# A Mamba stage with its last sums carried into the next round, two sets of semaphores, one block of Silu, and GpSimd two products ahead

## The reference, cut to what matters

```
hidden = layernorm(residual)
xin, z = split(hidden @ in_w.T)
xc = silu(causal_conv4(xin) + cb)
dtr, B, C = split(xc @ xp_w.T)
dt = softplus(dtr @ dtp_w.T + dtp_b)
h_t = exp(dt_t * A) * h_{t-1} + (dt_t * xc_t) * B_t     # A = -exp(A_log), for each state n
y_t = sum_n h_t[n] * C_t[n] + xc_t * D
residual = residual + (y * silu(z)) @ out_w.T
```

## Time and profile before

| what | us |
|---|---|
| median of three timed runs | 8238.78 (8215.06 to 8246.3) |
| the profiled execution | 8203.76 |
| its span | 8201.8 |
| busy in the span: TensorE, VectorE, ScalarE, GpSimd | 6408.0, 6500.0, 4681.8, 4525.0 |
| the Mamba rounds, from first to last scan and read-out | 107.87 to about 4081 |

### The profile page before, as it was taken

The page is one execution under the profiler, slowest core; times in us unless marked ns, Lnnn a source line. Parts: engine busy times, 40 slices in busy tenths (PEclk is TensorE's granted clock), DMA queues, the critical chain, the costliest instruction groups (busy, mean ns, idle before and its releaser), DMA issues. The chain is left out here.

```text
span 8201.8 us, 94294 instructions
## 1 busy us (share of the span) xinstructions
PE 6408.0 (78%) x25989; PEld 3374.8 (41%) x25989; DVE 6500.0 (79%) x15305; ACT 4681.8 (57%) x9323; POOL 4525.0 (55%) x2829
## 2 busy tenths in 40 slices
PE   5888888888888888888788867777556777777755
PEld 2333333333333333333355545555434444444522
DVE  5999989999899999999855558988667666666657
ACT  4666666666666666666555533433326666666633
POOL 4888888888888888888732335545211222222200
PEclk9999999999999999999977878888656777778755
DMA  5333333433433333343310047777310000000011
GB/s 183 143 154 152 149 140 151 161 139 155 156 142 154 149 152 145 146 161 138 147 33 27 21 129 209 215 210 211 104 45 14 10 10 10 10 10 10 7 34 36
DMA packets 373870, 896.58 MB, mean 109 GB/s; under 512 B 28169, under 2 KB 270214, under 8 KB 307110
## 3 DMA queue, kind: packets, MB, share of 16 engines
q1 hardware_dynamic: 332646, 692.64, 22.5%
q0 software_dynamic: 40960, 201.36, 8.5%
HBM read 850.57 MB, written 56.77 MB: 111 GB/s over the span
## 5 line engine op out<-in xcount | busy, mean ns | idle before, releaser
L365 POOL TENSOR_TENSOR mb_dBu<-mb_dtu,mb_rows_b 128x1024 f32<-128x1024 f32 x1027 | 2401.7, 2356 | 143.7 <-POOLq L63 98.9
L379 DVE TENSOR_TENSOR_SCAN mb_bank<-mb_bank,mb_dBu 128x1024 f32<-128x1024 f32 x704 | 1611.0, 2288 | 141.2 <-PEq L63 107.6
L350 ACT ACTIVATE mb_bank<-mb_dt,mb_a_neg 128x508 f32<-128x508 f32 x2050 | 1312.8, 671 | 2.3
L419 PE MATMUL mb_bank<-mb_hcd,ident 128*128 128x512 f32 x2560 | 1213.2, 607 | 25.1 <-DVE mb_hcd L393 25.0
L419 PE MATMUL mb_bank<-mb_hcp,ident 128*128 128x512 f32 x1280 | 856.3, 806 | 344.5 <-POOL mb_hcp L402 344.5
L402 POOL TENSOR_TENSOR mb_hcp<-mb_hs,mb_rows_c 128x1024 f32<-128x1024 f32 x320 | 750.9, 2347 | 479.8 <-DVE mb_hs L379 445.8
L393 DVE TENSOR_TENSOR mb_hcd<-mb_bank,mb_rows_c 128x1024 f32<-128x1024 f32 x704 | 861.8, 1224 | 32.3 <-PE mb_bank L419 0.7
L419 PEld LDWEIGHTS mb_bank<-mb_hcd,ident 128*128 128x128 f32 x2560 | 499.9, 200 | 753.9 <-issue 632.6
L379 DVE TENSOR_TENSOR_SCAN mb_hs<-mb_bank,mb_dBu 128x1024 f32<-128x1024 f32 x320 | 731.1, 2285 | 83.8 <-ACT mb_bank L350 83.8
L1523 POOL DMA_INDIRECT ex_rows<-in_ex_table,ex_idx x512 | 489.8, 957 | 523.9 <-DVE ex_idx L1519 310.4
L419 PEld LDWEIGHTS mb_bank<-mb_hcp,ident 128*128 128x128 f32 x1280 | 304.8, 253 | 777.8 <-POOL mb_hcp L402 412.6
(11 more groups left out here) (369 smaller groups left out, 12892.1 us busy)
## 6 DMA issues: line engine op xcount, KB each, us to landing
mb_rows_b<-bc_rows SPq DMA_DIRECT2D x259, 1024.0 KB, 7.6
mb_rows_c<-bc_rows SPq DMA_DIRECT2D x258, 1024.0 KB, 6.8
stream<-mb_r_post SPq DMA_DIRECT2D x69, 256.0 KB, 2.7
mb_r_tok<-stream SPq DMA_DIRECT2D x67, 256.0 KB, 2.7
mb_r_old<-stream SPq DMA_DIRECT2D x65, 256.0 KB, 2.8
ex_rows<-in_ex_table,ex_idx POOLq DMA_INDIRECT x512, 5.6
tj_x_tok<-stream SPq DMA_DIRECT2D x17, 256.0 KB, 3.1
bc_rows<-mb_xp SPq DMA_DIRECT2D x65, 64.0 KB, 1.6
```

Of the source, the lines that this page charges most:

```text
L350: e = nc.scalar.activation(da_of(n)[:, c * GB:(c + 1) * GB, 1:], dt[q][:, c].rearrange("p (b t) -> p b t", b=GB)[:, :, 1:], ACT.Exp, scale ...
L365: nc.gpsimd.tensor_tensor(by_c(dBu[m % RING][:]), by_c(chains(dtu[q][:])), over_c(rows_b[:, n]), ALU.mult).then_inc(s["mb_dbu"], 1)
L379: nc.vector.tensor_tensor_scan(flat(to), flat(da_of(n)), flat(dBu[n % RING][:]), 0.0, ALU.mult, ALU.add).then_inc(s["mb_scan"], 1)
L419: m = nc.tensor.matmul(bank[:, B_Y + c], ident[:], part[:, c * GB:(c + 1) * GB], start=False, stop=False)
```

## The change

- `pe_late_sums` takes the place of `pe_last_sum`: the sums of n = 13, 14 and 15 are left to the next round. So that their tiles are not written too early, the `hcd` tiles follow a table (`HCD`) and the two `hcp` tiles change places each round.
- `Turns` holds two sets of semaphores, used in turns. A round clears the other set at its start, on SyncE, with no barrier; the barrier at the block's end stays.
- The gate's product and Silu come right behind the convolution's Silu at n = 3, half by half; the x product moves to n = 0 in TensorE's order and waits for the gate's Silu (`mb_zg`), because it writes the same PSUM. The first half of the convolution moves to the end of the round before, behind the transposes.
- The gate on VectorE moves from n = 0 to n = 1, the new residual on ScalarE from n = 1 to n = 2, dt on VectorE from n = 10 to n = 11, dt * u on GpSimd from n = 11 to n = 12.
- The norm's statistics on VectorE move from n = 7 to n = 3; adding epsilon and the sign of the mean go from VectorE to ScalarE (`act_var`, n = 9), and the root on GpSimd from n = 9 to n = 10.
- GpSimd is two `dBu` ahead (`AHEAD`), the ring stays at four.

```diff
+AHEAD = 2
+LATE = 3
+HCD = (2, 0, 1, 2, 0, 1, 2, 0, 1, 0, 1)
...
+    def clear_other(self):
+
+        for first, end in self.sets[1 - self.q].runs:
+            self.nc.sync.sem_clear(range(first, end))
...
             def pe_x(self, pe):
-                pe.wait_ge(s["mb_u"], CH)
+                pe.wait_ge(s["mb_zg"], CH)
...
             def pe_z(self, pe):
-                pe.wait_ge(s["mb_dt"], 1)
                 for c in range(CH):
+                    pe.wait_ge(s["mb_u"], c + 1)
...
-            def pe_last_sum(self, pe):
...
+            def pe_late_sums(self, pe):
+                parts = (hcp[(len(ON_POOL) - 1 + self.q) % 2], hcd[HCD[-2]], hcd[HCD[-1]])
+                for i, part in enumerate(parts):
+                    for c in range(CH):
+                        m = nc.tensor.matmul(bank[:, B_Y + c], ident[:], part[:, c * GB:(c + 1) * GB], start=False,
+                                             stop=(i == len(parts) - 1))
+                    m.then_inc(s["mb_late"], 1)
...
-                if j >= 1:
-                    pool.wait_ge(s["mb_scan"], j)
+                if m >= RING:
+                    pool.wait_ge(s["mb_scan"], m - RING + 1)
...
                     for n in range(DS):
-                        scan.pool_dbu(pool, n + RING - 1, n)
+                        scan.pool_dbu(pool, n + AHEAD, n)
                         if n in ON_POOL:
                             scan.pool_read_out(pool, n)
-                        if n == 9:
+                        if n == 10:
                             pre.pool(pool)
-                        if n == 11:
+                        if n == 12:
                             ahead.pool_dtu(pool)
...
                         if n == 3:
                             for c in range(CH):
-                                ahead.act_conv(act, c)
+                                ahead.act_conv(act, c, 1)
+                            act.wait_ge(s["mb_yg"], 1)
+                            ahead.act_z(act)
...
-                    behind.pe_last_sum(pe)
-                    ahead.pe_conv(pe, 0)
+                    behind.pe_late_sums(pe)
                     behind.pe_out(pe)
+                    scan.pe_skip(pe)
                     pe.wait_ge(s["mb_new"], 1)
                     ahead.pe_conv(pe, 1)
-                    scan.pe_skip(pe)
-                    for n in range(DS - 1):
+                    ahead.pe_z(pe)
+                    for n in range(DS - 2):
...
-                            pe.wait_ge(s["mb_zg"], 1)
+                            pe.wait_ge(s["mb_dt"], 1)
                             pre.pe(pe)
-            s.clear()
+                    pe.wait_ge(s["mb_h"], 1)
+                    following.pe_conv(pe, 0)
```

More of the change, by code:

```diff
@@ L62, in clear, with __init__, __getitem__, use @@
             self.nc.sync.sem_clear(range(first, end))
+        self.nc.all_engine_barrier()
+class Turns:
+    def __init__(self, nc, stack, names):
+        self.nc = nc
+        self.sets = [Sems(nc, stack, [f"{n}_{q}" for n in names]) for q in range(2)]
+        self.q = 0
+    def __getitem__(self, name):
+        return self.sets[self.q][f"{name}_{self.q}"]
+    def use(self, q):
+        self.q = q
+    def clear_other(self):
+        for first, end in self.sets[1 - self.q].runs:
+            self.nc.sync.sem_clear(range(first, end))
+    def clear(self):
+        for one in self.sets:
+            for first, end in one.runs:
+                self.nc.sync.sem_clear(range(first, end))
         self.nc.all_engine_barrier()
@@ L145, in _ @@
                 nc.vector.memset(zg[1][:], 0.0)
-                nc.vector.memset(hcd[(len(ON_VECTOR) - 1) % 3][:], 0.0)
+                for part in hcd + hcp:
+                    nc.vector.memset(part[:], 0.0)
                 nc.vector.memset(w_out[:], 0.0)
                 nc.vector.memset(bank[:, B_DA:8], 0.0)
-        s = Sems(nc, ctx, ["mb_" + n for n in [
+        s = Turns(nc, ctx, ["mb_" + n for n in [
             "res", "rp", "store", "rows", "b0", "b1", "b2", "b3", "c0", "c1", "c2", "c3",
-            "stats", "norm", "xh", "tr", "h", "conv", "u", "xp", "xps", "dtp", "abs", "ey", "sq", "small", "ln", "poly", "log", "dt", "dtu", "z", "zg",
-            "dbu", "da", "scan", "hcd", "hcp", "sumd", "sump", "y", "yg", "out", "new", "raw", "weights", "wb", "skip", "wo", "apos", "aneg"]])
+            "stats", "var", "norm", "xh", "tr", "h", "conv", "u", "xp", "xps", "dtp", "abs", "ey", "sq", "small", "ln", "poly", "log", "dt", "dtu", "z", "zg",
+            "dbu", "da", "scan", "hcd", "hcp", "sumd", "sump", "late", "yg", "out", "new", "raw", "weights", "wb", "skip", "wo", "apos", "aneg"]])
         class Pre:
@@ L529, in _ @@
                 first.pe_dt(pe, True)
-                first.pe_z(pe)
-                pe.wait_ge(s["mb_zg"], 1)
+                pe.wait_ge(s["mb_dt"], 1)
                 again.pe(pe)
-        s.clear()
+                pe.wait_ge(s["mb_h"], 2)
+                Ahead(1).pe_conv(pe, 0)
         def round_of(layer, q, behind_at, ahead_at, shape=None):
-            pre, ahead, scan, behind = Pre(), Ahead(1 - q), Scan(q, 1 - q), Behind(1 - q)
+            s.use(q)
+            pre, ahead, following = Pre(), Ahead(1 - q), Ahead(q)
+            scan, behind = Scan(q, 1 - q), Behind(1 - q)
             with nc.Block() as block:
```

95 lines of the change are left out of this document (53 added, 42 removed).

## The result

The changed kernel took 8398.06 us, median of 4 runs (8375.73 to 8419.62), against 8235.0 for the kernel before, median of 4 on the same chip: a ratio of 1.0201 [1.0179, 1.0223]. It is 2% slower. The forecast was 8405 with a range of 8275 to 8465.

The account below looks back on a forecast made before the run. Waits bound the kernel: a chain from TensorE's dt product through scans 8 and 10 to GpSimd's tail. 56 x 2.8 + 8 x 1.4 + 7 = 175 us more gave 8405; range 8350 to 8460, opened to 8275 to 8465.

Parts of the forecast that it names:

- the chain: Each round: TensorE to the dt product, ScalarE's block, scan 8, scan 10, then GpSimd's tail of products.
- TensorE ahead of dt: Late sums and gate product ahead of the dt product, half a convolution less: dt ends 1.7 us later, at 28.4.
- The clock: Late sums at the round's start run at the low clock after TensorE's idle: gate held 1.4 us, round +2.8 in all.
- GpSimd's tail: Behind scan 10's product GpSimd owes eight operations at 2.30 to 2.33 and the root's 1.23: 19.8 us, ending at 62.4.
- Seam: Round's end: one of two barriers goes, 0.43 us (bounds 0 and 0.86); with TensorE's last sum, up to 1.3.
- dt later: VectorE's 1.55 us wait before dt goes, but GpSimd reaches dt's product only at about 50.7: nothing won.
- ScalarE: Two table loads of 1.28 us and a 2.59 us wait go; scan 8's exponential still waits for dt, 1.7 later.
- The other rounds and the single costs: Eight rounds building weights or skip matrices: +1.4 us each; prologue and last round: +7 us once.
- the signs named beforehand: Less VectorE idle before the first scan, GpSimd last, Abs at 28 to 30, no dt wait, slow late sums, four table loads.
- VectorE's four waits: Ordinary round before: 1.76 us at the end, 1.22 before scan 8, 0.18 before scan 10, 1.55 before dt.
- Rival C: Faster: relieved ScalarE starts its block from Abs sooner, scan 10 ends before 40.5; 120 us less, 8119; chance 0.11.

Follow-up runs that it names:

- the run with four products: The changed kernel with four unused products added on TensorE behind the half convolution at each round's end: 8358.64 us, ratio 1.0137.
- the run with two added products: The changed kernel with two unused products added on TensorE behind the half convolution at each round's end: 8330.25 us, ratio 1.0117.
- the run with the root moved: The changed kernel with epsilon and sign at n = 5 and GpSimd's root and shift at n = 9, ahead of scan 10's product: 8250.88 us, 1.0036.
- the seam-alone run: The kernel before with only the two sets of semaphores, one barrier a round, order of work kept: 8191.57 us, ratio 0.9953.
- the kernel with both mends: The changed kernel with GpSimd's root and shift ahead of n = 10's read-out and TensorE's first dt product at n = 2: 8074.87 us, 0.9822.

## Why the prediction was right

The direction, the size and the chain were right; single terms were off by a few tenths of a microsecond a round.

- **TensorE ahead of dt**, forecast +1.7: measured 3.37 for scan 10's end, of which 1.58 is the clock (Abs in the run with four products), so 1.79 by subtraction. The two rounds of the changed kernel with the clock up give the same: Abs at 28.60 against 26.81. Leaving the gate product out moved Abs and the round alike. (The prediction's own terms add up to 28.5 for the end of dt, not 28.4.)
- **The clock**, forecast +1.4 with some 3.4 us at half pace and the sums done at 7.0: in the round shown the three sums end at 7.09 and the gate starts at 7.13, on the mean 7.23, and the price is 1.58. The low clock was forecast from the first sum on; here it comes 1.00 us behind the start and costs the same. The slow products stand at the head of a chain, so 1.58 x 63 would be 100 us, 1.2% of 8398; that is an estimate, and the run with two added products had 68 us back, 0.8%. The Trainium skill ("TensorE: Matmul & The Clock Gate", Part 1: The HAM clock gate) puts the ramp at under 1% of a typical kernel's span, and speaks there of a kernel's start. Whether the price of a slow stretch in nearly every round lies above that figure is not shown by these runs.
- **GpSimd's tail**, forecast 19.8: 19.82 on the mean. The root behind scan 10's product was its added part, as the run with the root moved shows.
- **Seam**, forecast 0.43 for one barrier: 0.52 from GpSimd's end to the next scan, 0.39 less than before. In the trace of the seam-alone run only 0.17 an interval was had, since the last work ended later.
- **dt later**: the 1.55 us went, and the round got no shorter by it, as forecast: GpSimd takes up dt * u only at t = 52.5.
- **ScalarE**: four table loads, and Abs behind the dt product at once. The loads that went bought nothing in this round, for ScalarE waits 1.85 us longer for TensorE at the decisive place.
- **The other rounds and the single costs**: the 44 ordinary rounds give 133 of the 171 us, so the other 19 intervals give 38, +2.0 each, where eight at +1.4 and eleven at the ordinary +2.8 were forecast (42). The rounds as a whole were forecast at +168. The single costs were 7 in the forecast. The first round's scan starts 10 us later, and what follows the last round's first scan is 11 us longer. Not all of that is the change's: what follows the last round's first scan took 4181 to 4233 us in the traces of this study.

The sum came to 175 on the profiled execution against 192 measured, and on the medians to about 8410 against 8398. That the medians agree so closely is in part luck: the rounds cost a little more than forecast in the traces, and before's trace is a fast one.

Of the signs named beforehand one did not come, and Abs, at 30.2 on the mean, lies just outside its 28 to 30. VectorE's idle before the first scan was to be less; over the trace it grew from 107.6 to 186.2 us, as it must when GpSimd ends the rounds behind VectorE, the sign named next to it. (The list of VectorE's four waits also leaves out a fifth, 0.17 us ahead of scan 7; nothing hangs on it.)

The weak point was that clock and tail were priced apart. Moving the root, 1.23 us of GpSimd, gave back 2.54 a round.

Rival C was the kernel that this one could have been. Its condition, scan 10 before 40.5, was named; two moves by a few steps brought it about, though by another way than it named: Abs came earlier through TensorE's order, not through ScalarE's relief.

## What to carry to other kernels

Follow what is added to an engine up to the next thing that another engine waits for there, even where that engine is idle a fifth of the time: here 1.8 us ahead of dt was 1.8 us of the round, while 115 us less work for ScalarE brought no gain. Look at what stands behind the last wait on each engine, since a small operation there (a root of 1 us) is paid in full, and ahead of the wait for nothing. Time added at the end of a loop's round may be paid a second time, in the clock of the next one's first products: 1.23 us less there took 1.3 us off the wait for them.

## What was not expected of the hardware

- After the same idle of 1.90 us the half convolution took 3.70 us in one round and 5.40 in another of one trace. So the idle just before does not tell the clock alone.
- Idles of one length at the seam went either way: in the kernel with both mends 3.17 us without work left the late sum at full pace, and 3.16 led to one of 3.67 us. TensorE at the two seams, each with the half convolution ahead:

```profile
465.09 3.70 PE L241 MATMUL mb_bank<-mb_h_ch,mb_w_conv 128*128 128x512 f32 x8 [1.73 <-ACT mb_h_ch L230]
471.96 1.98 PE L329 MATMUL mb_bank<-mb_hcp,ident 128*128 128x512 f32 x4 [3.17 <-PEq L592]
...
698.88 3.70 PE L241 MATMUL mb_bank<-mb_h_ch,mb_w_conv 128*128 128x512 f32 x8 [1.90 <-ACT mb_h_ch L230]
705.74 3.67 PE L329 MATMUL mb_bank<-mb_hcp,ident 128*128 128x512 f32 x4 [3.16 <-PEq L592]
```

- The clock may fall after the work has begun again: in the changed kernel's round shown, 1.00 us into the late sums.

Why the half convolution and the late sums run slow in some rounds and not in others stays open.
